# Moving the receptance product of four steps from GpSimd to VectorE, and joining the scatters of a step in one row

## What is computed

```python
xn = layernorm(x)
# branch s: an RWKV layer (attention with a recurrence in time, then channel mixing)
h  = ln(xn)*ln1_w + ln1_b;  hx = shift(h)               # previous token of the same sequence
xk, xv, xr = (h*m + hx*(1-m) for m in (tmk, tmv, tmr))
k, v = xk @ att_kw.T, xv @ att_vw.T
sr   = sigmoid(xr @ att_rw.T)
rwkv = sr * wkv(time_decay, time_first, k, v)            # a weighted running mean over time
x2   = xn + rwkv @ att_ow.T
h2   = ln(x2)*ln2_w + ln2_b;  h2x = shift(h2)
kk   = square(relu(mix(h2, h2x) @ f_kw.T))
s    = x2 + sigmoid(mix(h2, h2x) @ f_rw.T) * (kk @ f_vw.T)
# branch g: a shared SwiGLU expert and one of 8 routed experts per token (top 1)
g    = silu(swiglu_shared(xn) + swiglu_routed(xn*score))
out  = x + s*g
```

## Time and profile before

| | |
|---|---|
| median of 3 runs | 498.06 us (495.76 to 499.38) |
| the profiled execution | 497.8 us |
| its span, first to last instruction | 495.9 us |
| mean granted TensorE clock | 0.988 |
| busy: PE, DVE, ACT, POOL | 444.2, 406.5, 355.9, 282.2 us |

### The profile page before, as it was taken

How to read it: one execution, slowest core, us unless ns; L and a number is a source line. 1 busy time by engine, 2 the same in 40 slices (tenths; PEclk the granted TensorE clock), 3 DMA queues, 4 the chain that set the end, 5 groups by cost and what they waited for, 6 DMA issues and landing times. The chain is left out here.

```text
span 495.9 us, 9005 instructions
## 1 busy us (share of the span) xinstructions
PE 444.2 (90%) x2663; PEld 332.7 (67%) x2663; DVE 406.5 (82%) x806; ACT 355.9 (72%) x716; POOL 282.2 (57%) x318
## 2 busy tenths in 40 slices
PE   1898998869989997799999999999999999988895
PEld 1667665547566663669686969687878787855562
DVE  4573969969799797979796979797988989789996
ACT  4868778564565657578787878787879697867891
POOL 7834685288787888427374655555555646470050
PEclk9999899898999999999999999999999999999999
DMA  8992000011511111225757565746573837209397
GB/s 255 273 275 51 2 0 1 5 45 57 190 35 48 46 33 51 55 81 151 212 156 214 172 208 171 232 138 206 147 237 108 226 101 224 79 19 291 106 123 217
DMA packets 66384, 64.97 MB, mean 131 GB/s; under 512 B 5952, under 2 KB 54465, under 8 KB 66256
## 3 DMA queue, kind: packets, MB, share of 16 engines
q1 hardware_dynamic: 58512, 53.52, 38.4%
q0 software_dynamic: 6960, 9.84, 7.3%
q10 hardware_dynamic: 864, 1.04, 0.7%
HBM read 46.86 MB, written 19.28 MB: 133 GB/s over the span
## 5 line engine op out<-in xcount | busy, mean ns | idle before, releaser
L1049 POOL DMA_INDIRECT routed_out<-xh,xs x71 | 93.1, 1312 | 45.2 <-ACT xh L809 30.5
L1041 POOL DMA_INDIRECT tokens_by_expert<-xn,pos x64 | 68.5, 1070 | 27.4 <-issue 27.4
L518 PEld LDWEIGHTS bank_ring<-xh,ew 128*128 128x128 f32 x568 | 70.2, 192 | 10.8 <-issue 9.7
L518 PE MATMUL bank_ring<-xh,ew 128*128 128x128 f32 x568 | 75.6, 276 | 1.0 <-ACT xh L809 0.5
L475 PE MATMUL bank_out<-fvw,kk 128*128 128x128 f32 x512 | 66.1, 277 | 0.0
L475 PEld LDWEIGHTS bank_out<-fvw,kk 128*128 128x128 f32 x512 | 62.0, 193 | 1.9 <-issue 1.9
L1318 DVE TENSOR_TENSOR kk<-rk 128x512 f32<-128x512 f32 x30 | 24.1, 804 | 40.9 <-ACT rk L767 40.7
L801 ACT ACTIVATE px<-bank_ring 128x256 f32<-128x256 f32 x71 | 27.1, 381 | 25.4 <-PE bank_ring L518 25.2
L532 PE MATMUL bank_ring<-ew,hx 128*128 128x128 f32 x284 | 43.5, 276 | 0.4 <-ACT xh L809 0.4
L532 PEld LDWEIGHTS bank_ring<-ew,hx 128*128 128x128 f32 x284 | 37.8, 193 | 0.6 <-ACT xh L809 0.6
L485 PEld LDWEIGHTS bank_ring<-sdn,hs 128*128 128x128 f32 x256 | 31.0, 192 | 10.3 <-issue 6.1
(11 more groups left out here) (198 smaller groups left out, 1096.8 us busy)
## 6 DMA issues: line engine op xcount, KB each, us to landing
ew<-ex_w SPq DMA_DIRECT2D x71, 384.0 KB
tokens_by_expert<-pad_row SPq DMA_DIRECT2D x1, 4686.0 KB, 21.1
xs<-tokens_by_expert SPq DMA_DIRECT2D x71, 66.0 KB, 3.0
xi<-x SPq DMA_DIRECT2D x12, 256.0 KB, 4.6
out<-xn SPq DMA_DIRECT2D x11, 256.0 KB, 4.0
ew<-routed_out SPq DMA_DIRECT2D x9, 256.0 KB, 4.4
out<-x SPq DMA_DIRECT2D x5, 256.0 KB
out<-xn POOLq DMA_DIRECT2D x5, 256.0 KB, 6.0
```

Source lines behind the costliest of these rows:

```text
L518: last = nc.tensor.matmul(part(GU[n % 2], q, P), part(w, q, P), xt[:, 0:P], start=True, stop=True)
L1041: nc.gpsimd.indirect_dma_start(xs_dram, bass.IndirectOffsetOnAxis(ap=POS[:, t:t + 1], axis=0), XN[:, t * XROW:(t + 1) * XROW], None).then_ ...
L1049: nc.gpsimd.indirect_dma_start(routed_dram, bass.IndirectOffsetOnAxis(ap=XS[(n - 2) % NXS][:, CH:CH + 1].bitcast(i32), axis=0), XH[n % NXH ...
```

## The change

In steps 1 to 4 GpSimd no longer makes the receptance product. VectorE makes it, with the function that it already had for chunks 0 and 15, between `running_max(i+1)` and `ffn_square(i-1, 3)`. GpSimd's scatters of a step then stand in one row: 10 in step 1, and 18 in each of the steps 2 to 4 (64 in all, as before). From step 5 on nothing changes.

```diff
@@ GpSimd, step(i)
                     pool.wait_ge(s_tok, 1)
-                    scatter(9)
+                    scatter(10)
                 elif 0 < i <= E_STEP:
-                    scatter(12)
+                    scatter(18)
                 for k in range(4, 8):
                     fill(i, k)
-                if T:
+                if T and i >= E_STEP:
                     make_rw(i)
-                if 0 < i < E_STEP:
-                    scatter(5)
@@ VectorE, step_one()
                 running_max(2)
+                make_rw(1)
                 ffn_square(0, 3)
                 differences(2)
@@ VectorE, step(i)
                 if P1:
                     running_max(i + 1)
+                if T and i < E_STEP:
+                    make_rw(i)
                 if C:
                     ffn_square(i - 1, 3)
```

## The result

| | kernel before | changed kernel |
|---|---|---|
| median, beside each other | 497.1 us (495.1 to 500.1, 20 runs) | 495.49 us (491.19 to 503.43, 20 runs) |
| ratio | | 0.9943, 95% interval 0.9916 to 0.9969 |
| profiled execution, its span | 497.8, 495.9 us | 495.65, 493.8 us |
| busy PE, DVE, ACT, POOL | 444.2, 406.5, 355.9, 282.2 us | 444.2, 404.9, 355.9, 278.3 us |

Medians are over all runs; a ratio compares only those runs of either kernel that lie within 1.5% of its fastest. The change gains 2.8 us by the ratio, and 7.0 were forecast; 495.49 lies 0.5 us above the range's upper end. In two later comparisons the same kernel had 0.9893 (0.9842 to 0.9944) and 0.9928 (0.9890 to 0.9966), with single runs between 490.4 and 496.6 us. In two more it was slower than the kernel before, 1.0181 and 1.0153; these are the disturbed comparisons further down.

A forecast was written before the change was run, and what follows sets the result against it. GpSimd's full list was taken to bound steps 1 to 4. Its shorter list (5.7 to 7.1 us) and earlier VectorE statistics (7.1 to 7.8) put z of step 5 7.0 earlier: 497.8 - 7.0 = 490.8 us, range 488.0 to 495.0.

The forecast's parts named there:

- What bounds the kernel: Steps 1 to 4: GpSimd's full list, waiting for nobody from 96.0 to 198.6, is on the path at both ends.
- Step 1 to 2: With the product on VectorE, attention_out starts 3.7 us earlier and make_x2 of step 2 3.5 us earlier, at 108.2.
- Steps 2 and 3: VectorE's product fits inside waits at no cost; squares shorten by 1.4 and 0.8 us; make_x2 comes 4.6 to 5.3 earlier.
- GpSimd comes to its x_sm of step 5 at 198.55 less 5.7: End of GpSimd's scatter stretch: without four products, x_sm of step 5 starts 5.7 to 7.1 us earlier.
- 0 to 0.7 us more a step and 0.3 as the value: Steps 2 to 4: time VectorE loses again per step to collisions with GpSimd's difference d and small instructions.
- up to 1.8: Step 5: further gain possible if GpSimd's small instructions, 4.5 us there, take the 2.7 of step 2.
- the shift reaches the end undiminished, minus 0 to 1 us: After step 5: z's 7.0 us gain carries through to the end, losing at most 0 to 1 us.
- (a): Three steps: GpSimd's small instructions and d take back 1 us each, gain 4.0, time 493.8; 0.16 together with (e).
- (b): Only step 1 gains, 3.5 us, because TensorE or VectorE then set the pace; 494.3 us; chance 0.08.
- (c): Larger gain of 9 us, with step 1's TensorE wait and lowered clock gone and short small instructions in step 5; 488.8; chance 0.10.
- (d): Slower: rows of 18 scatters back up beyond the twelfth, cancelling 7.0 us or reaching 505; 0.05 with any other loss.
- (e): Product stays on VectorE's path, without a wait to cover it; four times 0.6 us lost, 493.2; 0.16 together with (a).

The follow-up runs named there:

- paused: Changed kernel with three small unused GpSimd products between the twelfth and thirteenth scatter of steps 2 to 4; 503.18 us, ratio 1.0100 to the kernel before.
- pause_one: Changed kernel with one small unused GpSimd product between the twelfth and thirteenth scatter of steps 2 to 4; 498.19 us, ratio 1.0019 to the kernel before.
- d_only: Kernel before, its product still on GpSimd, with the difference d of chunks 3 to 5 moved to VectorE; 494.64 us, ratio 0.9939.
- again_c: Changed kernel unaltered, run and profiled once more; 494.17 us (491.62 to 496.59).
- again_b: Changed kernel unaltered, run and profiled once more; 492.59 us (490.39 to 493.74).
- micro_scatter: Separate program, not the kernel: GpSimd scatters and small products beside VectorE idle or running one instruction kind; scatter 0.97 us beside nothing, 1.14 beside two SBUF inputs.
- before_again: Kernel before, unaltered, run again for another profile; 495.13 us.
- d_on_vector: Changed kernel with the difference d of chunks 3 to 5 moved to VectorE too; 489.40 us, ratio 0.9843 to the kernel before.

## Why the prediction was wrong, and where it was right

**What bounds the kernel: right, but for step 3.** GpSimd's list is full through steps 2 to 4 and decides when x_sm of step 5 comes; paused, pause_one and d_only show it from both sides. Step 3 by itself was at the floor of 26.3 us already. One reading was wrong without harm: of the 27.4 us of "issue" that I put between the scatters, 9.2 lie ahead of the first.

**Step 1 to 2: right.** The product starts at 104.42 (forecast 105.04; the first scatter is 0.5 us earlier in this execution), attention_out at 106.16 (106.8), make_x2 at 107.53 (108.2).

**Steps 2 and 3: right in kind for make_x2.** The product costs VectorE nothing in step 2, the square is 0.69. make_x2 of steps 3 and 4 are 5.9 us earlier, more than I forecast (4.6, then 4.6 to 5.3); 0.5 us of it is the earlier first scatter, which is chance.

**The failed step: "GpSimd comes to its x_sm of step 5 at 198.55 less 5.7", "5.7 to 7.1 earlier".** It was 2.4 earlier (196.13), and 1.9 and 4.8 in again_c and again_b. Counted from the first scatter, the list is 1.9 us shorter, and 2.3 and 4.3 in these two. Of the 5.1 us that the product gave back, 1.2 went into longer scatters, 1.6 into longer small instructions and 0.4 into gaps. The term that should have held this, "0 to 0.7 us more a step and 0.3 as the value", I put on make_x2 alone; on GpSimd's own list I took collisions at nothing, and 1.26 us for every scatter, though the earlier trace rows had one of 1.27 us beside VectorE's square. 18 scatters of 1.26 are 22.7 us, and the row of step 3 took 26.0. Nor did I count what follows: a stretched instruction moves those behind it into further meetings. So x_sm of step 4 was 4.2 earlier, not "6 to 7". z of step 5, first in the changed kernel's first profile and then in again_b:

```profile
199.39 1.65 ACT L744 ACTIVATE z<-x,x_sm 128x128 f32<-128x128 f32 x4 [0.38 <-POOL x_sm L1029]
```

```profile
195.75 1.65 ACT L744 ACTIVATE z<-x,x_sm 128x128 f32<-128x128 f32 x4 [0.38 <-POOL x_sm L1029]
```

These are 3.6 and 7.3 us ahead of the 203.03 of the earlier trace rows. again_b's 7.3 beside the forecast's 7.0 is in part luck: its x_sm is only 4.8 us earlier, and the small instructions, 2.0 us where they had taken 4.5, give 2.5 where I allowed "up to 1.8".

The Trainium skill has the rule that I weighed only in its short form. "SBUF — State Buffer" (section "SBUF: two separate sides") says that the shared ports are an exclusive lock which whoever starts first holds for the whole instruction, and that descriptors written by GpSimd can be locked out by VectorE. The traces agree with the first in one direction: 0.01 us ahead of the scan a scatter took 0.96, 0.01 behind it 1.97. In the other they don't: the scan that started 0.01 behind the scatter took 1.25 and was not held, and the square of the earlier trace rows, which started 0.26 us ahead of GpSimd's product, was held all the same (2.09 for 0.69). For the second the page names VectorE's two-port performance mode; micro_scatter shows a longer issue beside two SBUF inputs (1.14 against 0.97), and no run here tells whether it is the writing of descriptors that waits or the reading of the positions (`pos`), which lie in SBUF.

**The other failed step: "the shift reaches the end undiminished, minus 0 to 1 us".** In again_b make_x2 of step 5 is 7.3 us ahead of the first profile of before, that of step 15 (449.03 against 455.17) 6.1, and the end of the span 4.8. Against before_again the three are 7.4, 3.5 and 2.2. In the changed kernel's first profile, against the first of before, they are 3.6, 2.1 and 2.1. So 1.2 to 3.9 us are lost in small pieces in the expert steps, which I did not follow, and why is open. again_b's 1.4 us behind them go where the clock dips. It does not dip there in any profile of before nor in the changed kernel's first one, so the changed order alone does not make it (before_again, then again_b, 21 us from make_x2 of step 15):

```profile
452.60:473.60 21.00, 18.17 (x89) 11.50 (x88) 19.20 (x44) 17.56 (x35) 6.25 (x8) 1.00 0.55 121
```

```profile
449.00:470.00 21.00, 18.43 (x86) 11.79 (x85) 17.89 (x42) 16.51 (x34) 4.83 (x7) 0.92 0.45 112
```

At 0.92 the 21 us hold 1.7 us less of clock.

**The base.** One profile stood for before, and its step 5 was the longest of three by 0.5 and 1.7 us. Its small instructions of step 5 took 4.5 us; in before_again they took 2.8. So the "up to 1.8 more" that I allowed as a gain comes without the change, in another execution.

**The rivals.** (a), 493.8, came nearest: right in kind (collisions give back 2.8 us on GpSimd's list), on its small instructions (1.6) and, which (a) had not, on scatters (1.2). (b) is refuted, since steps 2 to 4 have more to gain, as d_only and d_on_vector show; but TensorE and VectorE do set step 3, at 26.3 us. (c) had a clock dip that went in step 1, and dips came back elsewhere. (d)'s growing spacing is refuted; why rows of 16 to 18 scatters go with the slower kernels under the disturbance is open. (e) did not occur. No rival had the late hand-overs.

## What to carry to other kernels

Count a GpSimd instruction next to VectorE's instructions with two SBUF inputs at its own length and at that length plus the rest of VectorE's instruction, scatters included. Ask for each row how many such meetings there are, and remember that whatever moves a full list moves all its later meetings: the sum is a range of some us, and not one number. Work on such a list until it has slack: d_on_vector took one more us a step off it and gains 8.0 us where the change gained 4.8 beside it, with half the spread (six runs of each). Profile the kernel before more than once before you add up differences of a microsecond.

## What the runs showed of the hardware

- An indirect DMA's issue on GpSimd takes 0.96 us, and up to 2.14 (d_only) when a VectorE instruction with two SBUF inputs is under way at its start; it then ends 0.8 to 1.2 us behind that instruction. In three profiles 0.02 us of phase went with 0.96 or 1.97. One input in PSUM stretched none (micro_scatter).
- On a full GpSimd list such meetings add up: 5.4 us of pause made the list 11.3 us longer and the time 10.6. From d_on_vector to paused, 14.2 us of list went with 14.3 us of span.
- TensorE's granted clock was 0.63 for the 4 us behind a wait of 3.87 us (eight matmuls in 1.92 us for 1.06), and 1.00 with four matmuls for nothing in the wait; the time did not change by more than its interval.
- Under a disturbance that the profile doesn't explain, semaphores of TensorE's products counted up late, with waits of up to 10.1 us, in steps 2 to 4 only, and the sign of the change turned (0.989 to 1.018).
